# Fused attention and routing with batches run together and unread products ahead of PE's waits; loads of the heads attentions cut into pieces

## The reference, cut to what matters

```
# layer 1: attention with 8 heads of 16 channels at three scales, n = 1024, 256 and 64 tokens
attn = softmax(einsum('bhdn,bhdm->bhnm', q, k) / 16 ** 0.5)
out  = einsum('bhnm,bhdm->bhdn', attn, v)
...
# layer 2: t = t + attention(ln(t)), one head of 128 channels, then t = t + experts(ln(t))
W = einsum('bqd,bkd->bqk', Q, K) / scale
M = where(W == 0, 0, tril)
x_exp = exp(W - max(W)) * M
out = einsum('bqk,bkd->bqd', x_exp / (sum(x_exp) + 1e-9), V)
logits = x @ gate_w + gate_b
top_probs, top_idx = top_k(softmax(logits), 2)      # 2 of 16 experts for each token
...
# layer 3: 8 heads of 16 channels over 1024 tokens, with a bias for each head and key
scores = einsum('bihd,bjhd->bhij', q, k) / sqrt(hd) + col_bias[None, :, None, :]
```

## Time and profile before

| what | us |
|---|---|
| median of 3 runs (lowest and highest) | 2147.29 (2143.82 to 2149.95) |
| the profiled execution | 2145.99 |
| its span | 2144.1 |
| heads attentions of layer 1, about | 354.5 to 880 |
| fused attention and routing, about | 957 to 1224 |
| head_inputs and start of heads3, about | 1432 to 1512 |

### The profile page before, as it was taken

How to read it: one execution, slowest core, us unless ns; L and a number is a source line. 1 busy time by engine, 2 the same in 40 slices (tenths; PEclk the granted TensorE clock), 3 DMA queues, 4 the chain that set the end, 5 groups by cost and what they waited for, 6 DMA issues and landing times. The chain is left out here.

```text
span 2144.1 us, 29779 instructions
## 1 busy us (share of the span) xinstructions
PE 1690.9 (79%) x9116; PEld 861.6 (40%) x9116; DVE 1399.3 (65%) x2755; ACT 988.8 (46%) x1816; POOL 257.6 (12%) x272
## 2 busy tenths in 40 slices
PE   4998697997999965758776199633799999975798
PEld 3776342222232222335555088512122232225476
DVE  4752698886888857356665134365788888845566
ACT  2554232565677742014533066423167776762243
POOL 1010201000000000000221545410001100100000
PEclk9999897898999977779987599857599999996799
DMA  2270174084234100103000131219123222200000
GB/s 81 103 121 1 36 149 167 1 122 78 51 62 65 25 11 1 29 27 98 17 16 13 43 109 56 66 49 217 59 31 65 58 50 51 50 14 1 20 0 39
DMA packets 114817, 120.85 MB, mean 56 GB/s; under 512 B 22980, under 2 KB 88972, under 8 KB 113692
## 3 DMA queue, kind: packets, MB, share of 16 engines
q1 hardware_dynamic: 101118, 102.07, 21.4%
q0 software_dynamic: 13600, 17.58, 2.8%
HBM read 77.38 MB, written 41.75 MB: 56 GB/s over the span
## 5 line engine op out<-in xcount | busy, mean ns | idle before, releaser
L953 DVE TENSOR_REDUCE heads_mx<-heads_n_bank 128x1 f32<-128x1024 f32 (+2 forms) x536 | 625.3, 1206 | 148.1 <-PE heads_n_bank L836 144.5
L934 ACT ACTIVATE heads_prob<-heads_t_bank 128x512 f32<-128x512 f32 (+1 forms) x1064 | 549.6, 601 | 365.1 <-PE heads_t_bank L855 364.8
L836 PE MATMUL heads_n_bank<-scale_ks,scale_qs 96*128 96x512 bf16 (+2 forms) x608 | 182.4, 395 | 41.1 <-PEq L43 24.7
L836 PE MATMUL heads_n_bank<-edge_ks,edge_qs 99*128 99x512 bf16 x512 | 164.2, 405 | 52.3 <-PEq L43 41.0
L855 PE MATMUL heads_t_bank<-scale_qs,scale_ks 99*128 99x512 bf16 (+2 forms) x608 | 173.1, 373 | 18.4 <-DMA scale_qs<-heads_mrows 14.9
L869 PE MATMUL heads_o_bank<-heads_prob,scale_vs 128*32 128x512 f32 (+2 forms) x1216 | 152.5, 576 | 13.0 <-DVE scale_out L971 11.7
L855 PE MATMUL heads_t_bank<-edge_qs,edge_ks 102*128 102x512 bf16 x512 | 155.3, 382 | 3.8 <-ACT heads_prob L934 3.8
L869 PE MATMUL heads_o_bank<-heads_prob,edge_vs 128*32 128x512 f32 x1024 | 136.4, 605 | 0.1
L836 PEld LDWEIGHTS heads_n_bank<-scale_ks,scale_qs 96*128 96x128 bf16 (+1 forms) x608 | 49.0, 105 | 185.8 <-issue 102.7
L836 PEld LDWEIGHTS heads_n_bank<-edge_ks,edge_qs 99*128 99x128 bf16 x512 | 39.5, 99 | 187.5 <-issue 117.1
L855 PEld LDWEIGHTS heads_t_bank<-scale_qs,scale_ks 99*128 99x128 bf16 (+1 forms) x608 | 58.5, 103 | 121.4 <-ACT heads_prob L934 55.9
(11 more groups left out here) (331 smaller groups left out, 2555.8 us busy)
## 6 DMA issues: line engine op xcount, KB each, us to landing
edges_text<-edges_targets SPq DMA_DIRECT2D x16, 512.0 KB, 3.7
scale_qs<-scale_q_parts SPq DMA_DIRECT2D x60, 128.0 KB, 5.1
scale_ks<-scale_k_parts SPq DMA_DIRECT2D x60, 128.0 KB, 7.2
heads_wide<-heads_inverse_d POOLq DMA_DIRECT2D x14, 512.0 KB, 8.5
edge_qs<-edge_q_parts SPq DMA_DIRECT2D x48, 128.0 KB, 4.3
edge_ks<-edge_k_parts SPq DMA_DIRECT2D x48, 128.0 KB, 6.4
routed_x<-attn_zeros SPq DMA_DIRECT2D x2, 2600.0 KB
experts_xs<-routed_x SPq DMA_DIRECT2D x16, 325.0 KB
```

The costliest lines, as they stand in the source:

```text
L836: last = pe.matmul(ps[0:TN, at_:at_ + CH], query(b, slice(0, KB), s, h, j, t * TN, TN), key(b, slice(0, KB), s, j, i * CH, CH), start=True ...
L934: act.activation(to[:], t_ps[score_bank(of, place, g)[0]][0:TN, 0:HP * CH], ACT.Exp, scale=scale).then_inc(exped, 1)
L953: dve.tensor_reduce(mx[:, u % UC:u % UC + G], scores, AX.X, ALU.max, negate=True).then_inc(first_used, 1)
```

## The change

Three places are edited. (1) HeadsFirst.load loads one half at a time; in layer 3 the second half is loaded by SP at the start of heads3 and no longer within head_inputs. (2) HeadsEarly.load loads a piece (a group of batches, and q with v, or k); in heads0 SP issues one piece at each of g = 1 to 6. (3) attend_and_route runs its 32 tiles in one loop over all batches. Projections come in six chunks of 512 columns a batch, through halves of the bank of the turned probabilities, between tiles; q, k and v have two buffers; the weights have a semaphore of their own; ACT's normalisation and the routing parts are placed at other tiles, and note_pages moves from tile 7 of the following batch to tile 1 of the one after it. PE gets stay_busy: bf16 products of the identity with itself, 128 columns, into a bank that is written again afterwards. 8 of them stand ahead of each turn and 8 ahead of each mix, and 32, 16, 16 and 32 stand in the tail.

```diff
-    def load(self, sp):
-        for s in range(2):
-            self.load_qk(sp, 0, s, self.qk_loaded[s])
-            if s == 0:
-                sp.wait_ge(self.cleared, 2)
-                if self.bias_parts is not None:
-                    sp.dma_start(self.ks[STACK:STACK + 3, :], self.bias_parts.rearrange("l h n -> l (h n)")).then_inc(self.biased, 16)
-            self.load_v(sp, 0, s)
+    def load(self, sp, s):
+
+        self.load_qk(sp, 0, s, self.qk_loaded[s])
+        if s == 0 and self.bias_parts is not None:
+            sp.wait_ge(self.cleared, 2)
+            sp.dma_start(self.ks[STACK:STACK + 3, :], self.bias_parts.rearrange("l h n -> l (h n)")).then_inc(self.biased, 16)
+        self.load_v(sp, 0, s)
...
-    def load(self, sp):
+    def load(self, sp, i, j):
+
         n, LB = self.n, self.LB
...
+        part = slice(i * LB * n, (i + 1) * LB * n)
+        parts, dram, slots = ((self.qs, self.scratch.q, Q_PART), (self.ks, self.scratch.k, K_PART))[j]
+        for slot, level in enumerate(slots):
...
+        if j == 0:
             sp.dma_start(self.vs[:, i * LB:(i + 1) * LB], self.scratch.v[i * LB:(i + 1) * LB].rearrange("b p t c -> p b t c")).then_inc(self.v_loaded[i], 16)
...
             else:
+                if first.bias_parts is not None:
+                    first.load(sp, 1)
+                sp.wait_ge(cleared, 2)
+                pieces = [(one, i, j) for one in later for i in range(B // one.LB) for j in range(2)]
                 for g in range(2 * B):
...
-                    if 1 <= g <= len(later):
-                        later[g - 1].load(sp)
+                    if 1 <= g <= len(pieces):
+                        one, i, j = pieces[g - 1]
+                        one.load(sp, i, j)
...
                     sp.wait_ge(stored[0], 48)
-                    first.load(sp)
+                    for s in range(2):
+                        first.load(sp, s)
...
                 if b == 2:
-                    first.load(sp)
+                    first.load(sp, 0)
```

The core of attend_and_route, first PE:

```diff
+            def project(b, c):
+
                 if b > 0:
...
+                    pe.wait_ge(turn_kept, (b - 1) * T)
+                    pe.wait_ge(proj_kept, 6 * b + c)
+                elif c >= 2:
+                    pe.wait_ge(proj_kept, c - 1)
...
+            def stay_busy(bank, count):
+
+                for _ in range(count):
+                    pe.matmul(bank, m.identb[:], m.identb[:], start=True, stop=True)
+
+            def turn(g):
+                b, t = divmod(g, T)
+                if g >= 1:
+                    pe.wait_ge(turn_kept, g)
+                if t == 4 or g == 0:
+                    pe.wait_ge(proj_kept, 6 * min(b + 2, B) if g else 6)
+                stay_busy(t_ps[:, 0, :], 8)
+                pe.wait_ge(masked, g + 1)
                 for j in range(t + 1):
...
+            def mix(g):
+                b, t = divmod(g, T)
+                if g >= 1:
+                    pe.wait_ge(added, g)
+                stay_busy(mix_ps[:], 8)
+                pe.wait_ge(turn_kept, g + 1)
+                if t == 0:
+                    pe.wait_ge(proj_kept, 6 * b + 6)
+                for j in range(t + 1):
...
+            early, late = {0: 0, 1: 1, 2: 2, 3: 4}, {2: 3, 3: 5}
+            inside = {3: lambda f: turn_rows(f, 1), 4: gate_logits, 6: count_picks}
+
+            pe.wait_ge(w_loaded, WEIGHTS)
+            for c in range(6):
+                project(0, c)
             pe.wait_ge(loaded, LOADS)
             pe.wait_ge(prepared, 11)
...
+            scores(0)
+            scores(1)
+            for g in range(B * T):
+                b, t = divmod(g, T)
+                turn(g)
+                if g + 2 < B * T:
+                    scores(g + 2)
+                if b + 1 < B and t in early:
+                    project(b + 1, early[t])
+                if b >= 1 and t in inside:
+                    inside[t](b - 1)
+                mix(g)
+                if b + 1 < B and t in late:
+                    project(b + 1, late[t])
+                if b >= 1 and t == 1:
+                    turn_rows(b - 1, 0)
+            pe.wait_ge(added, B * T)
+            stay_busy(mix_ps[:], 32)
+            turn_rows(B - 1, 0)
+            stay_busy(mix_ps[:], 16)
+            turn_rows(B - 1, 1)
+            stay_busy(mix_ps[:], 16)
+            gate_logits(B - 1)
+            stay_busy(mix_ps[:], 32)
+            count_picks(B - 1)
```

Then ACT's and DVE's loops:

```diff
+            act.wait_ge(w_loaded, WEIGHTS)
+            for c in range(6):
+                keep_chunk(0, c)
+            exponentials(0)
+            exponentials(1)
+            for g in range(B * T):
+                b, t = divmod(g, T)
+                f = b - 1
+                if b >= 1 and t == 2:
+                    take_rows(f, 0)
+                keep_turned(g)
+                if b + 1 < B and t in early:
+                    keep_chunk(b + 1, early[t])
+                if g + 2 < B * T:
+                    exponentials(g + 2)
+                if b >= 1 and t == 3:
+                    take_rows(f, 1)
+                if b + 1 < B and t in late:
+                    keep_chunk(b + 1, late[t])
+                if b >= 1 and t == 0:
                     take_root(f)
+                    normalise(f, 0, 2)
+                elif b >= 1 and t == 1:
+                    normalise(f, 2, 4)
+                elif b >= 1 and t == 2:
+                    normalise(f, 4, 8)
+                elif b >= 1 and t == 4:
                     double(f)
...
-            beside = {0: (find_shift,), 4: (choose,), 5: (pick,), 6: (hand_out,), 7: (place_rows, note_pages)}
+            beside = {0: (find_shift,), 4: (choose,), 5: (pick,), 6: (hand_out,), 7: (place_rows,)}
...
+            maximum(0)
+            maximum(1)
+            mask(0)
+            for g in range(B * T):
+                b, t = divmod(g, T)
+                if g + 1 < B * T:
+                    mask(g + 1)
+                if g + 2 < B * T:
+                    maximum(g + 2)
+                invert(g)
+                add_output(g)
+                if g >= 1:
+                    measure(g - 1)
                 if b >= 1:
...
+                if b >= 2 and t == 1:
+                    note_pages(b - 2)
```

More of the change, by code:

```diff
@@ L1717, in attend_and_route @@
         w, tril = sb("w", [P, 3, C]), sb("tril", [P, P])
[L1718 removed]
+        q, k, v = ([sb(f"{x}{i}", [P, N]) for i in range(2)] for x in "qkv")
         neg, sums, inv = sb("neg", [P, T]), sb("sums", [P, T]), sb("inv", [P, T])
@@ new lines, in project @@
+                    pe.wait_ge(proj_kept, 6 * b + c)
+                elif c >= 2:
+                    pe.wait_ge(proj_kept, c - 1)
+                to, part = chunk_bank(b, c), slice(c % 2 * 512, c % 2 * 512 + 512)
+                if c < 4:
+                    last = pe.matmul(to.rearrange("p t c -> p (t c)"), w[:, c // 2, :], m.xnT[:, b, part], start=True, stop=True)
+                else:
+                    for t in range(4):
+                        last = pe.matmul(to[:, t, :], m.xnT[:, b, part][:, t * P:(t + 1) * P], w[:, 2, :], start=True, stop=True)
@@ new lines, in project, with scores @@
+                last.then_inc(projected, 1)
+            def scores(g):
+                b, t = divmod(g, T)
+                if t == 0:
+                    pe.wait_ge(proj_kept, 6 * b + 4)
+                if g >= 2:
+                    pe.wait_ge(exped, g - 1)
+                    pe.wait_ge(masked, g - 1)
+                for h in range(2):
+                    last = pe.matmul(s_ps[g % 2][:, h * 512:(h + 1) * 512], q[b % 2][:, t * P:(t + 1) * P], k[b % 2][:, h * 512:(h + 1) * 512], start=True, stop=True)
+                last.then_inc(scored, 1)
@@ new lines, in stay_busy @@
+            def stay_busy(bank, count):
[9 more added lines that the diff above has]
+                pe.wait_ge(masked, g + 1)
+                for j in range(t + 1):
+                    last = pe.transpose(t_ps[:, j, :], prob[g % 2][:, j * P:(j + 1) * P], m.ident[:])
+                last.then_inc(turned, 1)
@@ L1851, in _ @@
             pe.wait_ge(loaded, LOADS)
             pe.wait_ge(prepared, 11)
-            project(0, 0)
-            project(0, 1)
-            values(0)
-            for b in range(B):
-                pe.wait_ge(qk_kept, 2 * b + 2)
-                scores(b, 0)
-                scores(b, 1)
-                pe.wait_ge(v_kept, b + 1)
-                for t in range(T):
-                    pe.wait_ge(masked, b * T + t + 1)
-                    if t >= 1:
-                        pe.wait_ge(turn_kept, b * T + t)
-                    for j in range(t + 1):
-                        last = pe.transpose(t_ps[:, j, :], prob[t % 2][:, j * P:(j + 1) * P], m.ident[:])
-                    last.then_inc(turned, 1)
-                    if t + 2 < T:
-                        scores(b, t + 2)
-                    elif b + 1 < B:
-                        project(b + 1, t + 2 - T)
-                    mix(b, t)
```

(22 more changed lines are left out.)

163 lines of the change are left out of this document (56 added, 107 removed).

## The result

The change is worth 0.4%, not the 2.1% that I forecast. The changed kernel took 2140.91 us (median of 20 runs, 2135.0 to 2148.75), the kernel before 2150.14 us beside it (20 runs); the ratio is **0.9959**, 95% interval 0.9946 to 0.9972. The sign was right, the time lies above the range of 2080 to 2134 us.

The account below looks back on a forecast made before the run. No engine was full (PE 79%, DVE 65% busy), so the places were priced singly: 15.5 + 13 + 16 = 44.5 us off 2145.99 gives 2101.5, plus 1.3 to the median, 2103 us; range 2080 to 2134 us.

Parts of the forecast that it names:

- Loads in pieces, heads0: First heads attention: splitting 26 queued loads removes PE's 14.86 us wait for a row of maxima; gain 15.5 us.
- Second half of the loads moved: Ahead of heads3: 13 of 27 transfers leave the queue between the stores of batches 1 and 2; gain 13 us.
- Fused attention: order: Fused attention: each batch costs its fullest engine's need plus 1 us; with products and standstills 184.2 against 199.5 us.
- my signs: Expected in traces: 0.055 us product spacing, batch 0 over 34.8 us, PE near 90%, clock over 0.9 in batches 2 and 3.
- The products: Fused attention: unread products cost PE 0.055 us each, 7.0 us a batch, in the path where PE bounds.
- The standstill: Batches 2 and 3 of the fused attention: 5 us beside the scatter and 2 for a slow clock remain in each.
- Tail: After the fused attention's loop: added products outweigh faster logits; a loss of 1.2 us in all.
- Start: Start of the fused attention: projections wait for the three weights alone; gain 1.9 us.
- The products hide: Rival, fused attention: the products' 21 us in batches 1 to 3 fall into waits; 2082 us, chance 0.2.
- cost double: Rival, fused attention: products cost 0.11 us each, all on the path, 28 us more; 2131 us, chance 0.18.
- A load gain: Rival, heads0 or heads3: one load edit fails to pay, 13 to 15.5 us less; about 2117 us, chance 0.1.
- the edits to the order do nothing: Rival, fused attention: hand-over bubbles remain, gain 0 to -5 us; 2119 to 2124 us, chance 0.05.

Follow-up runs that it names:

- e2: Kernel before with the edits to the loads alone and the old fused attention: 2123.15 us, ratio 0.9885 to the kernel before.
- e12: Changed kernel with all products, 101 semaphore increments added to ACT, and the scatters of batches 0 and 1 paced in pairs: 2111.97 us, ratio 0.9832.
- e6: Changed kernel without the 608 unread products and with 101 semaphore increments added to ACT: 2113.24 us, ratio 0.9837 to the kernel before.
- e10: Changed kernel without products, with 101 semaphore increments on ACT and the scatters of batches 0 and 1 paced in pairs: 2096.13 us, ratio 0.9752.
- e3: Changed kernel, all products kept, with 101 semaphore increments added at the end of ACT's part of attend_and_route: 2125.46 us, ratio 0.9904.
- e7: Changed kernel with 101 semaphore increments on ACT and without the tail's 96 products, the loop's 512 kept: 2120.20 us, ratio 0.9878.
- e5: Kernel before with 24 semaphore increments added at the end of ACT's part of attend_and_route: 2157.98 us, ratio 1.0055.
- e8: Changed kernel without products, with 101 semaphore increments on ACT and all scatters issued behind the attention: 2148.77 us, ratio 1.0007.

## Why the prediction was wrong, step by step

- **Loads in pieces, heads0**: forecast 15.5, measured 14.8 us. Right in mechanism and size; the 14.86 us wait is gone from the list of waits. Over all traces the three attentions of layer 1 last 502.5 to 508.2 us with the pieces (eleven) and 519.1 to 522.9 without (three).
- **Second half of the loads moved**: forecast 13. The gap before heads3 is 13.8 us shorter, head_inputs itself 1.5 longer: 12.3. Right. e2 has both edits alone: 24.7 us by its ratio, 3.9 to either side, against a forecast of 28.5; 11.7 in heads0 and 13.7 in the gap by its trace.
- **Fused attention: order.** This step failed. "A batch should cost what its fullest engine needs", plus 1 us for overlap. PE's need was right: 39.7 + 43.9 + 43.9 + 38.7 = 166.2 us, and with the scatters paced, so without standstills, PE is busy 165.9 us in e12, at a clock of 0.97. The overlap was wrong: PE stands idle for 20 of the 186 us, where I allowed 4. A chain through PE, DVE and ACT bounds a step, not one engine. Without products the order gives 199.5 to 189.6 us (e6), 10 us; my forecast of 184.2 less four times 7.0 us of products would be 156.2, a gain of 43. Of my signs the spacing of 0.055 us and a batch 0 over 34.8 us came, PE near 90% and a clock over 0.9 in batches 2 and 3 did not: 80% and 76%, and 0.89 in both.
- **The products**: the price of one, 0.055 us, was right, and 4 of 7.0 us in batch 1 do hide, which I had given to a rival as an all or nothing. They are still a loss of 12.9 us in the body (e12 against e10). They did keep PE's clock up (batch 3: 0.96 in e12, 0.91 in e10), but the batches didn't get shorter by it.
- **The standstill**: I kept 5 us and 2 for the slow clock, twice, "whatever the cause". Pacing takes 13.2 us from the body of e3 (198.8 to 185.6) and 16.9 from e6's (189.6 to 172.7), where I had 14: right in size. The changed kernel's own profile has 205.5 with the same loop as e3, and e7 202.4, so one profile is good to some 3 us here, and by the worst of them the term was 6 too low.
- **Tail**: forecast -1.2, measured -4.7 (63.6 to 68.3). I priced the products by their own time; their cost is that the logits are read only when the scatter is over. Start: forecast 1.9, measured 3.8. Why the signal of the logits comes late behind such products isn't shown.
- **What no step had**: 9.6 us in heads3, from 24 more instructions of ACT in the stage of some 300 us earlier, and 3.4 in the experts. In my prediction the rule on crossing blocks served only to say that a standstill had another cause; what the same section of the Trainium skill ("Runtime: NRT & Kernel Launch", Instruction fetch mechanics) says about taken branches concerned this kernel more, and I costed nothing at places that the diff doesn't touch. The experts' loss is open: they take 141.6 to 146.0 us across the runs, with and without products, and 142.6 in e5, so the 24 instructions don't make it.

Of the rivals, none was the case. "The products hide" and "cost double" both spoke of their price; 3 of 7 us are paid in batch 1, and the spacing is 0.055. A load gain did not fail; the 9.6 us that heads3 lost look like it in the total, and only the comparison within heads3 tells the two apart. Nearest in size was "the edits to the order do nothing", which I gave 0.05: it had the fused attention at 0 to -5 us, and start, body and tail came to -6.9. But the order does do something, 10 us in e6; products and longer standstills took it back.

In sum, from the forecast of 44.5: heads3 -9.6, the body -21.3, the tail -3.5, the experts -3.4, head_inputs and what leads up to it -3.1 and the drift ahead of heads0 -1.5, the start +1.9, the loads and the end +1.0, is 5.0, the difference of the spans.

## What to carry to other kernels

A stage in which no engine is full (here PE, 140 of 173 us in e10) can be bounded by a chain through several engines, and then the sum of the fullest engine's work is no forecast: filling its idle time is only free as far as the filler ends before the wait does, and removing the idle time takes a shorter chain. After an edit compare the stages that it does not touch, product by product: a loop can start to refetch its instructions at each jump back when code ahead of it grows (here by 24), and padding in an idle stretch brings it back (here 101). Beside work that matters, issue indirect DMAs in pairs between its steps, not sixteen in a row.

## What the runs showed of the hardware that I had not expected

- Sixteen indirect scatters issued 1.26 us apart hold up other engines, in the changed kernel DVE by 4.9 to 9.4 us beyond its waiting for PE, though the DMA engines are busy only 13 to 17% of that time; in its tail DVE goes on 2.9 us behind the end of the last one (1182.93, then 1185.83). In pairs that start 4 to 8 us apart they hold up nothing that e8's lengths would show. What the engines lack meanwhile isn't shown. It isn't instructions: in the changed kernel none of their packets falls between 1046 and 1082, 1120 and 1143, or 1167 and 1200 us, around the ends of the three standstills. PE's products have no semaphore to wait for, and the releaser is named "remote".
- 24 instructions of padding in ACT's code ahead of heads3 make it 8 us longer, 27 don't: at each of two jumps back ACT stands for 4.4 to 4.7 us while four packets of instructions arrive.
